# Rotary tables in two steps, a second norm gathered in one slot, and another start of the first expert, in a two-layer attention and expert kernel on one core

## The chip, the core and the metric

The kernel runs on one core of a Trainium2 chip. A core has five engines with a queue of instructions each: PE (TensorE, matmuls and transposes, into PSUM), DVE (VectorE) and ACT (ScalarE) for arithmetic on SBUF and PSUM, POOL (GpSimd), and SP, which here only issues DMAs. Engines run side by side and wait for each other through semaphores. An instruction that waits holds up all that stands behind it in its own queue. The metric is the device time of one execution in microseconds (us), lower is better; it is given as the median of several runs.

## The reference

The input is `x`, 4 sequences of 512 rows of 512 numbers, and a context of 4 x 64 rows. Two layers follow each other, each an attention and a feed-forward part, each added to `x` through a gate:

```
x = x + tanh(g_xattn[0]) * L0_xattn(layernorm(x), ctx, ...)
x = x + tanh(g_ffn[0])   * L0_ffn(layernorm(x), ...)
x = x + tanh(g_xattn[1]) * L1_xattn(layernorm(x), ctx, mask, ...)
x = x + tanh(g_ffn[1])   * L1_ffn(layernorm(x), ...)
```

`L0_xattn` has 16 query heads and 4 key heads of 128. Queries and keys are normed, scaled by `q_norm_w` and `k_norm_w` and rotated: `q * cos + rotate_half(q) * sin`. The keys and values are those of the 64 context rows and, under a causal mask, of the 512 rows of the sequence itself. `L0_ffn` is a shared network plus a routed one: each of the 2048 rows goes to 4 of 16 experts, an expert takes up to 256 rows, and its weighted output is added to the row. The change lies in these first two parts and in what joins them. The second layer is not touched.

## The kernel before

`x` stays in SBUF as `x_res`, 16 tiles of 128 rows. The program is a chain of stages, and a stage ends with its semaphores cleared and a barrier of all engines (`Scope.clear`, line 98). Three stages matter here.

**`attention0_stage`** (names `a_...`). A step is one key head and one tile of rows, 4 x 16 = 64 steps, and the work of a step is spread over several *slots*. Slots are numbered from -3 to 65. Strings of words (`PE_ORDER`, `ACT_ORDER`, `DVE_ORDER`, `POOL_ORDER`, lines 133 to 159) say by hand what each engine does in a slot, and in which order. Slots -3 to -1 and the first are written out, the others go by the slot's number modulo 4. The words used below:

- `Z`, `C`, `c`, `H`, `G`: the context, in two batches 0 and 1. `C` multiplies a batch's rows into keys in a bank of `a_A`. On DVE `c` sums the squares (L654) and takes the keys out of the bank (L655). On POOL `c` is three instructions (L768, L770, L773) that make the norm. `H` turns the normed keys (L823), `G` makes the values (L817).
- `b`, `t` on DVE: `b` scales the keys' norm weight; `t` multiplies the loaded cosines and sines with the norm weights of keys and queries, two tables `a_cos_k`, `a_cos_q` (L645) and two tables `a_sin_k`, `a_sin_q` (L648, four instructions of 128 columns each), and casts the causal mask (L650).
- `k`, `q`: projections to key and value and to the queries, each number split into a high and a low half, so three matmuls for one (lines 120 to 122). The two banks of `a_A` are taken in turn by `C`, `k`, `q`, `G`, `V` and `W`. The first `q` takes the bank of the second `C`, and so waits for L655 of batch 1.
- `f` on ACT squares the queries (L599); `E` on DVE sums them (L713) and rotates (L714, L717); `q` on POOL norms and adds (L747 to L755); `K` and `T` on PE turn keys and queries (L904, L909).
- `A` on DVE (L616 to L620), `r` on POOL (L731), `X` on DVE (L629), `R` on PE (L830) and `r` on ACT (L515): the layer norm of a tile of `x`: sums, `rstd`, normed rows `a_xn`, transposes, and the copy into `xT`. `row(s, ahead, i)` says which tile is due in a slot. Tiles 0 to 3 are done at once in slot -3, tiles 4 to 15 one in a slot. Tile numbers 16 to 19 are the *second* norm, that of the first four tiles of `x` after this attention, for the next stage. They stand in slots 60 to 64, one in a slot, between the work of the last steps.
- `S`, `M`, `e`, `P`, `g`, `V`, `o`, `B`, `W`, `D`: scores, their maxima, exponentials, transposes of the probabilities and their copies, the product with the values, its split in two halves (L578 on ACT, L699 on DVE), the output projection, and the sum into `x` (L695).

**`ffn0_front_stage`** (`m_...`) computes the shared network and the routing, and writes the rows of `x` to `y_rows` in device memory. Its SP queue ends with waits for these writes (`y_stored`) and for the normed rows (`stored`).

**`experts_stage`** (`e_...`) runs 16 experts. ACT copies an expert's weights into a high half `e_whi` in three pieces (gate, up, down; L1673), POOL makes the low halves `e_wlo` of gate and up (L1503), DVE that of down (L1735). PE turns the gathered rows into `e_TR` (L1540), ACT and DVE split them (`split_x`, L1679 and L1728), and the matmuls into `e_GUP` follow. For the first expert the queues are filled by these lines of ACT:

```
                for j in range(NW):
                    split_hi(0, j)
                split_x(0)
```

Of the kernel before, what the change touches and what calls it, by code (L numbers as in the profile page):

```python
# [24 lines left out]
F32 = mybir.dt.float32  # L25
# [99 lines left out]
def attention0_stage(nc, x, ident, tri, gates, xT, xh, xl, next_weights, next_loaded, xn_dram, x_in, ctx_in, wq_in, wk_in, wv_in, wo_in, wkc_in, wvc_in, qw_in, kw_in, g_xattn, g_ffn,  # L125
# [7 lines left out]
    PE_ORDER = {-3: "Z0 Z1 R0 R1 R2 R3 C0 C1",  # L133
# [10 lines left out]
    ACT_ORDER = {-3: "z0 z1 r0 r1 r2 r3 x u w c0",  # L144
# [13 lines left out]
    POOL_ORDER = {-3: "r0 r1 r2 r3 x w c0", -2: "x c1 r", -1: "q x r", "first": "x q p0 p1 r",  # L158
# [15 lines left out]
    def steps(order, s):  # L174
        return [(word[0], int(word[1:] or 0)) for word in order[s if s < 0 else s % BT if s > 0 else "first"].split()]
# [91 lines left out]
    with ExitStack() as ctx:  # L267
# [99 lines left out]
        with nc.Block() as block:  # L367
# [133 lines left out]
            def _(act):  # L501
# [3 lines left out]
                def do(name, i, s, m):  # L505
# [99 lines left out]
            def _(ve):  # L605
                ve.memset(mhalf[:], -0.5).then_inc(tab_ready, 1)
                ve.memset(heps[:], HD * 1e-6).then_inc(tab_ready, 1)
                def do(name, i, s, m):
# [12 lines left out]
                    if name == "X" and row(s, 5, i) is not None:  # L621
# [19 lines left out]
                    if name == "t":  # L641

                        ve.wait_ge(tab_loaded, 48)
                        for q, wr in (("k", kw[:]), ("q", wrow[:, 0])):
                            ve.tensor_tensor(cw[q][:], cw["q"][:], wr.unsqueeze(1).broadcast_to([P, BT, HD]), ALU.mult).then_inc(tab_ready, 1)  # L645
                            swapped = wr.rearrange("p (s d) -> p s d", s=2)[:, ::-1, :]
                            for t in range(BT):
# [1928 lines left out]
```

## Time and profile before

| | |
|---|---|
| median of 3 runs | 1999.44 us (1999.3 to 1999.74) |
| the profiled execution | 1994.72 us |
| its span, first to last instruction | 1992.9 us |
| PE busy (share of the span) | 1852.5 us (93%) |
| DVE busy | 1099.0 us (55%) |
| ACT busy | 1038.4 us (52%) |
| POOL busy | 962.9 us (48%) |

The shares are means over all stages. The profile is read by stretch: a table of the engines' busy time in a stretch, the instructions in order of time, and for each of them the idle time of its engine just before and what ended it. An idle time of PE that ends with another engine's instruction names the chain that was late there.

### The profile page before, as it was taken

How to read it: one execution, taken by the hardware profiler on the slowest of the kernel's cores; microseconds unless marked ns; L12 is line 12 of the kernel's file. 1: busy time of each engine (PE TensorE's matmuls, PEld its weight loads, DVE VectorE, ACT ScalarE, POOL GpSimd, SP SyncE). 2: the span in 40 equal slices, each digit the busy share in tenths (PEclk: the TensorE clock that was granted, in tenths of full speed). 3: DMA queues.
4: the chain of work that ended last, by engine and by line, in shares of the span. 5: the costliest groups of instructions: out<-in, count | busy, mean ns of one | idle time of the engine just before them, and what ended most of it. 6: DMA issues, size and time to landing. Idle time of an engine off the chain costs nothing. (4 is left out here: it accounts for less than half of the span.)

```text
span 1992.9 us, 27633 instructions
## 1 busy us (share of the span) xinstructions
PE 1852.5 (93%) x9796; PEld 1323.4 (66%) x9796; DVE 1099.0 (55%) x2264; ACT 1038.4 (52%) x2251; POOL 962.9 (48%) x865
## 2 busy tenths in 40 slices
PE   6999999999999999999998999989999778859998
PEld 4666766766766666666765877769999656624443
DVE  4544544446455654556444648424343678748886
ACT  3555656554554545544544321126666367647775
POOL 4544565444653445544531100028888355537774
PEclk8999999999999999999999999989999989979999
DMA  7111111111012111111011100147889750000000
GB/s 235 45 50 50 48 34 47 62 31 50 34 33 71 48 52 47 34 49 39 25 47 67 65 22 22 43 144 203 233 226 273 184 134 1 1 0 23 21 18 27
DMA packets 112952, 141.18 MB, mean 71 GB/s; under 512 B 37408, under 2 KB 68128, under 8 KB 112624
## 3 DMA queue, kind: packets, MB, share of 16 engines
q1 hardware_dynamic: 105648, 122.63, 19.6%
q0 software_dynamic: 7168, 16.78, 4.0%
q8 instruction: 80, 1.31, 0.3%
q14 instruction: 56, 0.46, 0.1%
HBM read 104.78 MB, written 29.36 MB: 67 GB/s over the span
## 5 line engine op out<-in xcount | busy, mean ns | idle before, releaser
L743 POOL TENSOR_TENSOR a_xcl<-xT,a_xch 128x512 fp32r<-128x512 f32 x64 | 82.4, 1287 | 322.9 <-ACT a_xch L558 322.9
L898 PE MATMUL a_A<-a_pT,a_vf 128*128 128x512 f32 (+1 forms) x448 | 236.7, 610 | 0.9 <-ACT a_pT L574 0.9
L848 PE MATMUL a_S<-a_kT,a_qT 128*128 128x288 f32 (+3 forms) x640 | 209.7, 426 | 4.8 <-ACT a_qT L586 3.1
L659 DVE TENSOR_REDUCE a_nmax<-a_S 128x1 f32<-128x192 f32 (+3 forms) x256 | 138.1, 551 | 83.2 <-PE a_S L849 81.9
L564 ACT ACTIVATE a_pr_odd<-a_S,a_nmax 128x320 f32<-128x320 f32 (+1 forms) x128 | 80.9, 633 | 156.1 <-DVE a_nmax L659 154.8
L120 PE MATMUL a_A<-a_wlo,a_xch 128*128 128x512 f32 x256 | 153.7, 600 | 6.3 <-DVE a_qT L655 6.3
L848 PEld LDWEIGHTS a_S<-a_kT,a_qT 128*128 128x128 f32 x640 | 114.8, 189 | 53.8 <-issue 26.8
L574 ACT ACTIVATE a_pT<-a_TR 128x512 f32<-128x512 f32 (+1 forms) x224 | 132.3, 591 | 33.0 <-PE a_TR L888 32.2
L2404 PE MATMUL f_HH<-w12T,f_f_xqT 128*128 128x512 bf16 x512 | 125.0, 394 | 14.8 <-DVE f_h L2261 13.0
L564 ACT ACTIVATE a_pr_even<-a_S,a_nmax 128x192 f32<-128x192 f32 (+1 forms) x128 | 67.0, 525 | 135.1 <-DVE a_nmax L659 135.0
L1503 POOL TENSOR_TENSOR e_wlo<-expert_raw,e_whi 128x1408 fp32r<-128x1408 f32 x32 | 102.8, 3232 | 68.0 <-ACT e_whi L1673 68.0
L699 DVE TENSOR_TENSOR a_otl<-a_A,a_oth 128x512 fp32r<-128x512 f32 x64 | 44.2, 691 | 152.1 <-ACT a_oth L578 152.1
L120 PE MATMUL a_A<-a_wlo,a_oth 128*128 128x512 f32 x256 | 111.4, 435 | 7.3 <-DVE a_otl L699 7.2
L120 PE MATMUL e_GUP<-e_xgl,e_whi 128*128 128x256 f32 (+1 forms) x384 | 110.8, 289 | 5.2 <-DVE e_xgl L1728 4.5
L121 PE MATMUL e_GUP<-e_xgh,e_wlo 128*128 128x256 f32 (+1 forms) x384 | 109.3, 285 | 0.0
L122 PE MATMUL e_GUP<-e_xgh,e_whi 128*128 128x256 f32 (+1 forms) x384 | 108.7, 283 | 0.0
L2041 POOL TENSOR_TENSOR f_hg<-f_h,g 128x512 f32<-128x512 f32 x64 | 81.4, 1272 | 51.8 <-DVE f_h L2261 51.8
L122 PE MATMUL a_A<-a_whi,a_xch 128*128 128x512 f32 x256 | 102.2, 399 | 0.0
L121 PE MATMUL a_A<-a_whi,a_xcl 128*128 128x512 f32 x256 | 102.0, 398 | 0.0
L122 PE MATMUL a_A<-a_whi,a_oth 128*128 128x512 f32 x256 | 101.6, 397 | 0.0
L121 PE MATMUL a_A<-a_whi,a_otl 128*128 128x512 f32 x256 | 101.1, 395 | 0.0
L684 DVE RECIPROCAL a_rec<-a_rs 128x1 f32<-128x1 f32 x256 | 41.3, 161 | 107.7 <-ACT a_pr_odd L564 57.6
(389 smaller groups left out, 5193.3 us busy)
## 6 DMA issues: line engine op xcount, KB each, us to landing
a_pw<-in_L_ffn_w_dram SPq DMA_DIRECT2D x96, 256.0 KB, 2.8
expert_raw<-in_L_ffn_w_gate_dram SPq DMA_DIRECT2D x16, 704.0 KB, 7.9
expert_raw<-in_L_ffn_w_up_dram SPq DMA_DIRECT2D x16, 704.0 KB, 9.8
expert_raw<-in_L_ffn_w_down_dram SPq DMA_DIRECT2D x16, 512.0 KB, 10.2
tern<-a_tern SPq DMA_DIRECT2D x48, 128.0 KB, 1.9
x_res<-in_x_dram SPq DMA_DIRECT2D x4, 1024.0 KB, 9.3
a_raw<-in_L_xattn_wq_dram SPq DMA_DIRECT2D x4, 1024.0 KB, 6.5
a_raw<-in_L_xattn_wo_dram SPq DMA_DIRECT2D x4, 1024.0 KB, 5.5
```

The source lines that it names most:

```text
L120: pe.matmul(out, lhs_hi, rhs_lo, start=first, stop=False)
L121: pe.matmul(out, lhs_lo, rhs_hi, start=False, stop=False)
L122: return pe.matmul(out, lhs_hi, rhs_hi, start=False, stop=last)
L564: act.activation(pr[s % 2][:, i, 0:keys(s)], pair(s, i), ACT.Exp, bias=nmax[:, s % 2, i:i + 1], accum_out=rs[:, s % 2, i:i + 1]).then_inc( ...
L574: act.activation(pT[0:rows(i), i % 2], TR[0:rows(i), TR_USE["P", t, i][0]], ACT.Copy).then_inc(pT_ready, 1)
L659: ve.tensor_reduce(nmax[:, s % 2, i:i + 1], pair(s, i), AX.X, ALU.max, negate=True).then_inc(s_max, 1)
L743: pool.tensor_tensor(xcl[:, t % 2], xT[:, :, tok(t)], xch[:, t % 2].bitcast(F32), ALU.subtract).then_inc(xlo_ready, 1)
L848: pe.matmul(bank[:, lo:hi], qT[:, t % 2, hq], kT[:, par(t), lo:hi], start=True, stop=hi < nk)
L898: last = pe.matmul(A[:, A_USE["V", t, 0][0]], vf[r, par(t), i], pT[r, i % 2], start=i == 0, stop=i == nkt - 1)
L1503: pool.tensor_tensor(wlo[e % 2][q, cs], raw[q, e % 2, cs], whi[e % 2][q, cs].bitcast(F32), ALU.subtract).then_inc(gu_lo, 1)
L2041: pool.tensor_tensor(hg[:, u, part(n)], h[:, u, part(n)], g3[:, part(n)], ALU.mult).then_inc(hg_ready, 1)
L2404: last = pe.matmul(HH[pair_of(s, n)][j][:], f_xqT[:, u, j * KD + k], w12T[j][:, k, part(n)], start=k == 0, stop=k == KD - 1)
```

## The change

There are four parts.

1. **Tables.** The word `t` is split into `t0` (keys) and `t1` (queries and mask). `t0` stands ahead of `c1` as before, `t1` behind it. The four sine instructions of a table become one of 512 columns. In slot -2 DVE's order `v E A` becomes `v A E`.
2. **Second norm.** Slot 64 gets an order of its own, `"last"`, in which all four tiles 16 to 19 are normed. Slots 60 to 63 have none of it. The transposes go into the score banks `a_S` instead of `a_TR`, and DVE copies them into `xT` instead of ACT.
3. **Stores of the front stage.** `y_stored` outlives the stage. The waits at the end of its SP queue are gone; SP and POOL wait for `y_stored` in the experts' stage, where they first need it.
4. **First expert.** ACT splits the rows after the first weight piece instead of after the third. DVE makes the low half of the gate piece, and POOL only that of the up piece.

```diff
-    PE_ORDER = {-3: "Z0 Z1 R0 R1 R2 R3 C0 C1",
+    PE_ORDER = {"last": "W0 W1 W2 W3 R0 P0 P1 V0 R1 P2 V1 P3 V2 R2 P4 V3 R3 V4", -3: "Z0 Z1 R0 R1 R2 R3 C0 C1",
...
-    ACT_ORDER = {-3: "z0 z1 r0 r1 r2 r3 x u w c0",
+    ACT_ORDER = {"last": "g0 g1 g2 g3 g4 o L", -3: "z0 z1 r0 r1 r2 r3 x u w c0",
...
-    DVE_ORDER = {-3: "A0 A1 X0 A2 X1 A3 X2 X3 b u c0 t c1", -2: "v E A", -1: "v X E A", "first": DVE_SLOT,
+    DVE_ORDER = {"last": "A0 A1 X0 D X1 r0 A2 X2 r1 A3 X3 r2 r3 B", -3: "A0 A1 X0 A2 X1 A3 X2 X3 b u c0 t0 c1 t1", -2: "v A E", -1: "v X E A", "first": DVE_SLOT,
...
+                    if name == "r":
+                        t = row(s, 5, i)
+                        ve.wait_ge(xn_turned, t + 1)
+                        ve.wait_ge(xlo_ready, SLOTS)
+                        ve.tensor_copy(xT[:, :, tok(t)], S[:, i].rearrange("p (k t) -> p k t", k=KD)).then_inc(xT_ready, 1)
...
-                            for t in range(BT):
-                                ve.tensor_tensor(sw[q][:, t], sw["q"][:, t], swapped, ALU.mult).then_inc(tab_ready, 1)
+                        ve.tensor_tensor(sw[q][:], sw["q"][:], swapped, ALU.mult).then_inc(tab_ready, 1)
...
-                        bank = bank_of_TR("R", t, 0, s, m)
+                        if s == SLOTS:
+                            pe.wait_ge(s_exp, GH * SLOTS)
+                            bank = S[:, i]
+                        else:
+                            bank = bank_of_TR("R", t, 0, s, m)
...
-                for r in range(RING):
-                    sp.wait_ge(stored[r], 16 * (NT - BT) // RING)
-                sp.wait_ge(y_stored, 16 * (NT + 2 * NS))
...
+                sp.wait_ge(y_stored, 16 * (NT + 2 * NS))
                 for e in range(2, E):
...
-                    for j in range(2):
+                    for j in (1,) if e == 0 else range(2):
                         pool.wait_ge(whi_ready, NW * e + j + 1)
+                        pool.wait_ge(gu_lo, 2 * e + j)
...
+                    else:
+                        pool.wait_ge(y_stored, 16 * (NT + 2 * NS))
...
-                for j in range(NW):
+                split_hi(0, 0)
+                split_x(0)
+                for j in range(1, NW):
                     split_hi(0, j)
-                split_x(0)
...
+                ve.wait_ge(whi_ready, 1)
+                for q, cs in pieces(0):
+                    ve.tensor_tensor(wlo[0][q, cs], raw[q, 0, cs], whi[0][q, cs].bitcast(F32), ALU.subtract).then_inc(gu_lo, 1)
                 split_x(0)
```

DVE in the opening, before: `a_ssc` and `a_qT` are the `c` of one batch, `a_kT` is where the loaded mask lies, the instructions with `a_ssq` and behind it are `E`, and `a_stats` to `a_veps` are `A`.

```order
L645 TENSOR_TENSOR a_cos_k<-a_cos_q,a_kw 128x512
L648 TENSOR_TENSOR a_sin_k<-a_sin_q,a_kw 128x128 x4
L645 TENSOR_TENSOR a_cos_q<-a_cos_q,a_sq 128x512
L648 TENSOR_TENSOR a_sin_q<-a_sin_q,a_sq 128x128 x4
L650 CAST a_causal<-a_kT 128x128
L654 TENSOR_REDUCE a_ssc<-a_pr_even 128x4
L655 TENSOR_TENSOR a_qT<-a_A,a_kw 128x512
L704 TENSOR_TENSOR a_qa<-a_A,a_cos_k 128x128
L706 TENSOR_TENSOR a_qb<-a_A,a_sin_k 128x128
L713 TENSOR_REDUCE a_ssq<-a_sq 128x5
L714 TENSOR_TENSOR a_qa<-a_A,a_cos_q 128x512
L717 TENSOR_TENSOR a_qb<-a_A,a_sin_q 128x512
```

The same place on DVE in the changed kernel:

```order
L652 TENSOR_TENSOR a_cos_k<-a_cos_q,a_kw 128x512
L654 TENSOR_TENSOR a_sin_k<-a_sin_q,a_kw 128x512
L661 TENSOR_REDUCE a_ssc<-a_pr_even 128x4
L662 TENSOR_TENSOR a_qT<-a_A,a_kw 128x512
L652 TENSOR_TENSOR a_cos_q<-a_cos_q,a_sq 128x512
L654 TENSOR_TENSOR a_sin_q<-a_sin_q,a_sq 128x512
L657 CAST a_causal<-a_kT 128x128
L711 TENSOR_TENSOR a_qa<-a_A,a_cos_k 128x128
L713 TENSOR_TENSOR a_qb<-a_A,a_sin_k 128x128
L617 BN_STATS a_stats<-x_res 128x6
L619 BN_AGGR a_mv<-a_stats 128x2
L621 TENSOR_SCALAR a_veps<-a_mv 128x1
```

The second batch of the context moved ahead of the query tables and the mask, and `A` ahead of `E`.

PE in slot 64, behind its `W`, before: `a_pr_odd` rows are `P`, `a_vf` rows are `V`, the `a_xn` row is the `R` of tile 19.

```order
L888 MATMUL a_TR<-ident_f,a_pr_odd 128x128 x4
L830 MATMUL a_TR<-ident_f,a_xn 128x128 x4
L888 MATMUL a_TR<-ident_f,a_pr_odd 128x128 x4
L898 MATMUL a_A<-a_pT,a_vf 128x512
L888 MATMUL a_TR<-ident_f,a_pr_odd 128x128 x4
L898 MATMUL a_A<-a_pT,a_vf 128x512
L888 MATMUL a_TR<-ident_f,a_pr_odd 128x128 x4
L898 MATMUL a_A<-a_pT,a_vf 128x512
L888 MATMUL a_TR<-ident_f,a_pr_odd 128x128 x4
L898 MATMUL a_A<-a_pT,a_vf 128x512 x2
```

The same place on PE in the changed kernel:

```order
L841 MATMUL a_S<-ident_f,a_xn 128x128 x4
L899 MATMUL a_TR<-ident_f,a_pr_odd 128x128 x8
L909 MATMUL a_A<-a_pT,a_vf 128x512
L841 MATMUL a_S<-ident_f,a_xn 128x128 x4
L899 MATMUL a_TR<-ident_f,a_pr_odd 128x128 x4
L909 MATMUL a_A<-a_pT,a_vf 128x512
L899 MATMUL a_TR<-ident_f,a_pr_odd 128x128 x4
L909 MATMUL a_A<-a_pT,a_vf 128x512
L841 MATMUL a_S<-ident_f,a_xn 128x128 x4
L899 MATMUL a_TR<-ident_f,a_pr_odd 128x128 x4
L909 MATMUL a_A<-a_pT,a_vf 128x512
L841 MATMUL a_S<-ident_f,a_xn 128x128 x4
```

Three groups of transposes came in from slots 61 to 63, where nothing stands in their place.

ACT at the start of the experts, before (`expert_raw` are the loaded weights):

```order
L1673 ACTIVATE e_whi<-expert_raw 128x1408 x2
L1673 ACTIVATE e_whi<-expert_raw 128x1024
L1673 ACTIVATE e_whi<-expert_raw 96x512
L1679 ACTIVATE e_xgh<-e_TR 128x4x128 x2
L1698 ACTIVATE e_sil<-e_GUP 128x256
```

The same place on ACT in the changed kernel:

```order
L1685 ACTIVATE e_whi<-expert_raw 128x1408
L1691 ACTIVATE e_xgh<-e_TR 128x4x128 x2
L1685 ACTIVATE e_whi<-expert_raw 128x1408
L1685 ACTIVATE e_whi<-expert_raw 128x1024
L1685 ACTIVATE e_whi<-expert_raw 96x512
L1711 ACTIVATE e_sil<-e_GUP 128x256
```

The split of the rows moved ahead of the up and down pieces.

## Rows read from the trace of the kernel before

**Rows 1.** Stretches: length, busy us (instructions) per engine, PE's granted clock, DMA share, GB/s
```profile
80.00:1010.00 930.00, 913.11 (x4456) 642.49 (x4455) 485.19 (x1068) 502.12 (x1264) 452.57 (x445) 1.00 0.15 47
...
44.40:47.80 3.40, 3.38 (x11) 2.87 (x11) 0.00 (x0) 1.19 (x2) 0.44 (x1) 0.51 0.05 14
```

**Rows 2.** DVE in time, opening: start, us, line, output<-inputs, count [idle <-releaser]
```profile
20.41 0.68 DVE L645 TENSOR_TENSOR a_cos_k<-a_cos_q,a_kw 128x512 f32<-128x512 f32 x1
21.01 3.06 DVE L648 TENSOR_TENSOR a_sin_k<-a_sin_q,a_kw 128x128 f32<-128x128 f32 x4
...
28.16 0.68 DVE L655 TENSOR_TENSOR a_qT<-a_A,a_kw 128x512 f32<-128x512 f32 x1
...
21.01 1.38 DVE L648 TENSOR_TENSOR a_sin_k<-a_sin_q,a_kw 128x128 f32<-128x128 f32 x1
```

**Rows 3.** PE and ACT in time, opening
```profile
28.90 0.79 PE L120 MATMUL a_A<-a_wlo,a_xch 128*128 128x512 f32 x1 [6.34 <-DVE a_qT L655]
...
34.88 0.60 ACT L599 ACTIVATE a_sq<-a_A 128x512 f32<-128x512 f32 x1 [1.57 <-PE a_A L122]
...
37.68 0.67 PE L817 MATMUL a_A<-a_pT,a_pr_even 128*128 128x512 f32 x1 [0.96 <-DVE a_qb L717]
...
43.66 0.33 PE L904 MATMUL a_TR<-ident_f,a_qa 128*128 128x128 f32 x1 [2.32 <-POOL a_qa L755]
```

**Rows 4.** POOL in time, opening
```profile
20.43 1.81 POOL L738 TENSOR_TENSOR a_wlo<-a_raw,a_whi 128x512 fp32r<-128x512 f32 x1
...
22.20 1.31 POOL L738 TENSOR_TENSOR a_wlo<-a_raw,a_whi 128x512 fp32r<-128x512 f32 x1
...
25.09 1.09 POOL L773 TENSOR_TENSOR a_qT<-a_qT,a_src 128x512 f32<-128x512 f32 x1
...
38.61 0.56 POOL L731 TENSOR_TENSOR a_rstd<-a_veps,a_mhalf 128x1 f32<-128x1 f32 x1 [7.81 <-DVE a_veps L620]
...
42.35 1.25 POOL L755 TENSOR_TENSOR a_qa<-a_qa,a_srq 128x640 f32<-128x640 f32 x1
```

**Rows 5.** Issue of x's second batch, in time, and its landing, KB, us
```profile
17.12 0.47 SPq L394 DMA_DIRECT2D x_res<-in_x_dram  x1
...
x_res<-in_x_dram SPq DMA_DIRECT2D x1, 1024.0 KB, 8.2
```

**Rows 6.** Slots 61 to 65: group (count, busy us, mean ns, idle before), then in time
```profile
L830 PE MATMUL a_TR<-ident_f,a_xn 128*128 128x128 f32 x16 | 2.6, 283 | 2.3 <-DVE a_xn L629 2.3
...
1067.53 0.68 DVE L616 BATCH_NORM_STATS2 a_stats<-x_res 128x6 f32<-128x512 f32 x1
...
1068.70 0.56 POOL L731 TENSOR_TENSOR a_rstd<-a_veps,a_mhalf 128x1 f32<-128x1 f32 x1 [8.52 <-DVE a_veps L620]
...
1079.19 0.60 ACT L578 ACTIVATE a_oth<-a_A 128x512 fp32r<-128x512 f32 x1 [1.22 <-PE a_A L898]
```

**Rows 7.** Last store of the front stage, in time, and its landing, KB, us
```profile
1326.33 0.32 SPq L1027 DMA_DIRECT2D y_rows<-x_res  x1
...
y_rows<-x_res SPq DMA_DIRECT2D x1, 256.0 KB, 2.0
```

**Rows 8.** Start of the experts in time; last, a subtraction of the front stage
```profile
1329.49 4.11 ACT L1673 ACTIVATE e_whi<-expert_raw 128x1408 fp32r<-128x1408 f32 x4 [19.80 <-PEq L100]
1329.51 1.94 PE L1540 MATMUL e_TR<-ident_f,xg 128*128 128x128 f32 x8 [4.00 <-PEq L100]
1330.95 6.27 POOL L1503 TENSOR_TENSOR e_wlo<-expert_raw,e_whi 128x1408 fp32r<-128x1408 f32 x2 [47.79 <-ACT e_whi L1673]
...
1334.59 1.29 DVE L1728 TENSOR_TENSOR e_xgl<-e_TR,e_xgh 128x512 fp32r<-128x512 f32 x2 [8.29 <-ACT e_xgh L1679]
...
1335.94 0.58 PE L120 MATMUL e_GUP<-e_xgl,e_whi 128*128 128x256 f32 x1 [4.49 <-DVE e_xgl L1728]
...
1341.46 0.38 ACT L1698 ACTIVATE e_sil<-e_GUP 128x256 f32<-128x256 f32 x1 [6.90 <-PE e_GUP L122]
...
1086.55 3.30 DVE L1216 TENSOR_TENSOR m_gl<-xT,m_gh 128x704 fp32r<-128x704 f32 x4 [0.71 <-ACT m_gh L1157]
```

More of the change, by code:

```diff
@@ L174, in steps @@
     def steps(order, s):
-        return [(word[0], int(word[1:] or 0)) for word in order[s if s < 0 else s % BT if s > 0 else "first"].split()]
+        kind = s if s < 0 else "first" if s == 0 else "last" if s == SLOTS else s % BT
+        return [(word[0], int(word[1:] or 0)) for word in order[kind].split()]
     def batch_next(s):
@@ L184, in row @@
             return i
-        n = s + ahead
-        return n if BT <= n < PERIOD else n - AGAIN if PERIOD <= n - AGAIN < PERIOD + BT else None
+        if s == SLOTS:
+            return PERIOD + i
+        return s + ahead if BT <= s + ahead < PERIOD else None
     def bank_order(firsts):
@@ L197, in bank_order @@
                 elif name == "R":
-                    if row(s, 5, i) is not None:
+                    if s < SLOTS and row(s, 5, i) is not None:
                         taken.append((name, row(s, 5, i), 0))
@@ L509, in do @@
                                        ACT.Copy).then_inc(ctx_copied, 1)
-                    if name == "r" and row(s, 5, i) is not None:
+                    if name == "r" and s < SLOTS and row(s, 5, i) is not None:
                         t = row(s, 5, i)
                         act.wait_ge(xn_turned, t + 1)
-                        if t >= PERIOD:
-                            act.wait_ge(xlo_ready, SLOTS)
                         act.activation(xT[:, :, tok(t)], TR[:, TR_USE["R", t, 0][0]].rearrange("p (k t) -> p k t", k=KD),
@@ L641, in do @@
                     if name == "t":
[L643 to L646, printed above, removed]
[L647 to L651 removed]
+                        if i == 0:
+                            ve.wait_ge(tab_loaded, 48)
+                        q, wr = (("k", kw[:]), ("q", wrow[:, 0]))[i]
+                        ve.tensor_tensor(cw[q][:], cw["q"][:], wr.unsqueeze(1).broadcast_to([P, BT, HD]), ALU.mult).then_inc(tab_ready, 1)
+                        swapped = wr.rearrange("p (s d) -> p s d", s=2)[:, ::-1, :].unsqueeze(1).broadcast_to([P, BT, 2, HD // 2])
+                        ve.tensor_tensor(sw[q][:], sw["q"][:], swapped, ALU.mult).then_inc(tab_ready, 1)
+                        if i == 1:
+                            ve.wait_ge(causal_loaded, 16)
+                            ve.tensor_copy(causal[:], causal_in).then_inc(tab_ready, 1)
+                            ve.wait_ge(tab_ready, TABLES)
                     if name == "c":
```

23 lines of the change are left out of this document (10 added, 13 removed), and 2 rows, old and new, of the table ACT_ORDER.

## The prediction

> **What bounds the kernel now.** I read the table of stretches first, then PE's instructions in time with the idle time ahead of each, then for each idle time the instruction that ended it, on its own engine. From 80 to 1010 us PE is busy 913.11 of 930 us at a full granted clock [rows 1]: nothing is to be had there, and the change doesn't touch it. What it touches are three places where PE stands still.
>
> *Opening.* PE waits 6.34 us for L655, ready only at 28.84 because DVE does all the tables ahead of it [rows 2, 3]. It waits again, 2.32 us, until 43.66, for POOL's last instruction on the first queries [rows 3]. POOL began that chain at 39.17, behind an `rstd` for which it had waited 7.81 us; the DVE sums under that `rstd` stand behind `E` [rows 4]. Right after this idle time PE's clock was granted at 0.51, the 1.2 GHz level, from 44.4 to 47.8 [rows 1].
>
> *Last slots.* In slots 61 to 65 PE waits 2.3 us in all for normed rows of the second norm [rows 6].
>
> *From front stage to experts.* The last row store is issued at 1326.33 and lands 2.0 us later, at 1328.33; only then does SP reach the barrier [rows 7], and ACT and PE begin at 1329.49 [rows 8]. PE's first expert matmul starts 6.45 us after that: ACT first copies all three weight pieces (4.11 us), then splits the rows, and DVE follows [rows 8].
>
> **Part 1, the tables.** DVE does the key cosines at 20.41 (0.68 us for 512 columns). The first sine piece of 128 columns, at 21.01, took 1.38 us, until 22.39; POOL's weight chunk had ended at 22.24 [rows 2, 4]. I read this as DVE held until the chunk was over. One sine instruction of 512 columns is in neither kernel's trace so far. Not held it would end at 21.7; held as the first piece was, and then as long as the cosine one, at 22.9; as long as the four together at 24.07. I take 22.9, the nearest row being the same operation at the same place. POOL's fourth chunk (1.31) then ends at 24.2 instead of 23.51. `c1` follows on DVE, two instructions of 0.68 with some overlap, 1.3 in all: the bank is free at 24.2, and PE goes on at 24.25 instead of 28.90, **4.65 us sooner**.
>
> From there the chain is the old one. PE's restart to `f` on ACT took 34.88 - 28.90 = 5.98: `f` at 30.25. `G0` followed `f` by 2.80: at 33.05. It took 43.66 - 2.32 - 37.68 = 3.66 [rows 3]: PE could start `K` at 36.7. POOL must be as quick: from its fourth chunk to the end of the first batch's norm took 26.18 - 23.51 = 2.67 [rows 4], so 26.9; a subtraction of a chunk's size, 1.3, to 28.2; the second batch, again 2.67, to 30.9; the `rstd`, 0.56, to 31.45, since its sums now stand ahead of `E`. The query chain starts with DVE's sum behind `f`: 30.25 + 0.60 + an estimated 0.85 (640 columns at the rate of 0.68 for 512) = 31.7. It took 42.35 + 1.25 - 39.17 = 4.43 [rows 4], which gives 36.15. So `K` comes at 36.75 instead of 43.66: **6.9 us**, with PE's second idle time gone.
>
> Then the clock. The 3.4 us at 0.51 would be 1.7 at the full clock. The idle time just ahead of them is gone, but another, of some 0.4, stands at 30.5. I take 1.1 of the 1.7, between none and all. **Opening: 8.0 us**, bounds 4.6 (only the first idle time) and 9.2 (all of the clock, and a little of the matmuls behind 28.90 that ran slow).
>
> What the swapped `A` adds is a wait of DVE for `x`'s second batch, with `E` queued behind it and POOL and PE behind that. It is issued at 17.12 and lands 8.2 later, at 25.3 [rows 5]; DVE gets there at about 26.5. No cost. The query tables and the mask (two of 0.68 and a cast) run from 24.2 to about 26 and are needed by `f` at 30.25: hidden, with 4 us to spare.
>
> **Part 2, the second norm.** PE does the same 16 transposes of 283 ns [rows 6], only later, and ACT's four copies become four on DVE (0.68 each by L655, which reads PSUM too). So PE's work is neither more nor less, and what goes are the waits, 2.3 us, and some 0.2 for banks that the transposes shared with the probabilities: **2.5 us**, if slot 64 makes no new wait. There DVE does per tile the sums (1068.70 - 1067.53 = 1.17 until POOL can start), POOL 0.56 [rows 6], then `X` (an estimated 0.55) and the copy 0.68: about 3.0 us in a row for a tile. The first `X` stands ahead of `D` and is ready 1.17 + 0.56 + 0.55 = 2.3 after the slot's start, the second, behind `D`, at an estimated 4.3, and the fourth at about 4.3 + 2 x 3.0 = 10.3. PE comes to the fourth transposes behind V3. In the old slot `o` started 11.66 after the start [rows 6], so V3 ended near 10.5 less the old wait, plus the two groups of transposes put in: near 10.7. The margin is 0.4 us. Behind the fourth stand V4, `o`, `B` and the last `W`, all on the path. `X2` and `X3` also wait for the stores of `X0` and `X1`; at 2.0 for such a store [rows 7] these land at about 5.1 and 6.7, ahead of need. Bounds: 0.8 (DVE 1.7 late) to 3.2.
>
> **Part 3, the stores.** The barrier came 1329.49 - 1328.33 = 1.16 ahead of the next stage's work [rows 7, 8]. Now SP is free when its last issue ends, 1326.65, so work starts at 1327.81: 1.68 less, I take **1.6**, bounds 1.0 and 1.7. SP's new wait stands ahead of the load of the third expert, POOL's ahead of its first add; both come later than 1328.33 by more than the time of a store. No cost.
>
> **Part 4, the first expert**, counted from the start of ACT [rows 8]. Gate piece: 4.11 us are for 4352 columns, so 1408 take 1.33. The transposes end at 1.96; ACT splits the rows by 3.0 (it took 1334.59 - 1333.60 = 1.0). DVE makes the gate's low half from 1.33: 704 columns took 0.83, so 1.65, to 3.0, while POOL is idle; then `split_x`, 1.29, to 4.3. PE starts at 4.35 instead of 6.45. Up piece: ACT from 3.0 to 4.35, POOL 3.13 more, 7.5. PE's first group took 5.52 from its start to ACT's L1698, half of it gate: 2.76, so at 7.1 PE waits 0.4 for up. Gain 2.1 - 0.4 = 1.7; less if these matmuls are a little quicker and the wait longer: **1.5**, bounds 0.5 and 2.1. DVE's down piece now waits behind POOL, but is needed only by the second product, several us later.
>
> **Sum.** 8.0 + 2.5 + 1.6 + 1.5 = 13.6 us off the profiled execution's 1994.72: 1981.1. The median of the runs is 1999.44, 4.7 above that execution, and I take the difference off it: **1985.8 us**. All four places are ahead of barriers or on a chain through PE, and the loads in between are started by progress, not by the clock on the wall, so I expect no later place to take the gain back.
>
> **Rivals.**
>
> *POOL becomes the bound of the opening.* The chunk that began just as DVE did its cosines took 1.81, the next 1.31 [rows 4]: a DVE instruction held POOL for 0.5. In the new order the two query tables and the cast run beside POOL's norm of the context. Three times 0.5 puts `K` 1.5 later, PE waits again, and the clock falls as before (1.1): opening 5.4, time 1988.4. Against it: POOL's chain ends 0.6 ahead of need. Chance 0.16. The Trainium skill (SBUF — State Buffer, Who interferes with whom) says that a VectorE instruction with two SBUF inputs holds GpSimd's reads of SBUF for its whole length, and that issue order decides who waits. By that the three would cost 0.68 each, 2.0 in all, and the time would be 1988.9; the trace agrees in kind, with 0.5 for 0.68.
>
> *The norms crowd slot 64.* DVE's chain is late by 2.5 us, through `X` waiting for a port or a store, and `o` with it: part 2 gives nothing, 1988.3. For it: a margin of 0.4. Against it: POOL has nothing else to do there. Chance 0.10.
>
> *The sine instruction does not do what it should*: held again in between, it ends at 24.07. Then PE restarts 1.2 later, 1987.0. Chance 0.06.
>
> *Two of these at once, and a smaller part missing too*: a gain under 4.0 us, about 1996. Chance 0.04.
>
> *Slower than before*: DVE waits in `A` for `x`'s second batch with `E` behind it. `E` is due at 30.85 and `A` takes 1.2, so from a landing after 29.7 on each us costs one. It uses up all 13.6 at a landing at 43.3; at 48 the time is 2004. It landed at 25.3 [rows 5]. Chance 0.02.
>
> **How the numbers follow.** My forecast has 0.62, the rivals the rest. The time is the forecast's, 1985.8. The bounds of the terms give 16.2 us at best (1983.2) and 6.9 at worst (1992.5). The range runs from 1983.2 to 1991.2, which takes in the first three rivals, the first two together as well (1990.9), and leaves out less than 2 in 10. A measurement of this kernel can tell 0.2%, 4.0 us, from no change. Faster by more: 0.62 + 0.16 + 0.10 + 0.06 = 0.94, of which I give 0.01 to within, for a forecast that fails wholly: 0.93; within: 0.04 + 0.01 = 0.05; slower: 0.02.
>
> **What would show it.** Right: PE's first long idle time ends near 24.2, on L662; `K` starts near 36.7 with little or no wait on POOL; no wait of PE for `a_xn` in slots 61 to 63, and `o` of slot 64 about 12 us after the slot's start; 2.5 us instead of 4.0 of idle PE ahead of `e_TR`; PE's first expert matmul 4.35 after ACT's start, with a short wait before the up half. Wrong: PE idle ahead of `K` as long as before, or ahead of V4 or the last `W`; a wait of DVE for `x` in the opening; a first group of the expert that waits for POOL by more than 1.5.

## The result and the profile after

| | before | changed |
|---|---|---|
| first comparison, median | 1999.59 us (4 runs, 1999.30 to 1999.99) | 1983.91 us (4 runs, 1979.17 to 1984.32) |
| all runs whose clock is on record, mean | 1997.5 us (58 runs, 1991.5 to 2001.7) | 1983.4 us (10 runs, 1979.2 to 1985.3) |
| mean granted clock of PE over those runs | 0.9752 | 0.9781 |

The ratio of the first comparison is 0.9916 (0.9899 to 0.9933), a gain of 16.8 us (13.4 to 20.2). Over the runs of the second row the gain is 14.1 us, with an interval of 1.3 to either side. The forecast was 13.6 and 1985.8. The direction was right; by the first ratio the time is 0.9916 x 1999.44 = 1982.6, 0.6 under the lower end of the range (the ten runs' mean, 1983.4, lies just inside it). Both kernels turned out to have a spread of 6 to 10 us, of which the three runs shown of before had told nothing.

The profiled execution of the changed kernel took 1984.32 us (span 1982.5). PE, opening, in time order: start, length, line, output<-inputs, count, and in brackets the idle time just before and what ended it.

```profile
24.99 0.50 PE L120 MATMUL a_A<-a_wlo,a_xch 128*128 128x512 f32 x1 [2.63 <-DVE a_qT L662]
...
30.61 0.66 PE L830 MATMUL a_TR<-ident_f,a_qT 128*128 128x128 f32 x4 [0.54 <-POOL a_qT L780]
32.90 1.96 PE L824 MATMUL a_A<-a_pT,a_pr_even 128*128 128x512 f32 x4 [0.20 <-DVE a_qb L724]
...
36.41 0.27 PE L915 MATMUL a_TR<-ident_f,a_qa 128*128 128x128 f32 x1
...
40.77 0.49 PE L859 MATMUL a_S<-a_kT,a_qT 128*128 128x192 f32 x2
```

The 6.34 us ahead of 28.90 [rows 3] have become 2.63 ahead of 24.99, and the 2.32 ahead of `K` are gone: `K` (L915) starts at 36.41 instead of 43.66, 7.25 sooner (forecast 6.9). A new short wait stands at 30.61, for POOL's norm of the second batch of the context. DVE and POOL in the same stretch:

```profile
20.29 1.77 DVE L652 TENSOR_TENSOR a_cos_k<-a_cos_q,a_kw 128x512 f32<-128x512 f32 x1
21.99 1.75 DVE L654 TENSOR_TENSOR a_sin_k<-a_sin_q,a_kw 128x512 f32<-128x512 f32 x1
...
28.64 0.68 DVE L617 BATCH_NORM_STATS2 a_stats<-x_res 128x6 f32<-128x512 f32 x1
```

```profile
20.23 1.28 POOL L745 TENSOR_TENSOR a_wlo<-a_raw,a_whi 128x512 fp32r<-128x512 f32 x1
...
30.52 0.56 POOL L738 TENSOR_TENSOR a_rstd<-a_veps,a_mhalf 128x1 f32<-128x1 f32 x1
```

The one sine instruction took 1.75, as near to a held one as was forecast, but the cosine ahead of it, 0.68 before [rows 2], took 1.77. `A` (L617) ran without a wait for `x`, and the `rstd` at 30.52 had nothing to wait for, where it had waited 7.81 [rows 4]. PE's clock was not full here either: it was granted at 0.51 from 25.5 to 28.8, behind the wait of 2.63.

Slots 61 to 65, PE's transposes of normed rows as a group (count, busy us, mean ns, idle ahead), and the table of two stretches (length, busy time of PE, PEld, DVE, ACT and POOL, granted clock, DMA share, GB/s):

```profile
L841 PE MATMUL a_S<-ident_f,a_xn 128*128 128x128 f32 x16 | 2.5, 276 | 0.0
```

```profile
1056.30:1059.60 3.30, 3.30 (x10) 2.52 (x9) 1.91 (x7) 0.00 (x0) 1.37 (x2) 0.51 0.15 48
...
1060.36:1076.03 15.67, 11.81 (x59) 7.57 (x57) 10.46 (x18) 5.36 (x8) 1.10 (x2) 1.00 0.14 52
```

The 2.3 us of waiting [rows 6] are 0.0. But for 3.3 us at the start of slot 64 PE's clock was at 0.51, the 1.2 GHz level, which it was not in the trace of before.

From the front stage into the experts, in time:

```profile
1317.05 0.32 SPq L1037 DMA_DIRECT2D y_rows<-x_res  x1
1318.45 1.38 ACT L1685 ACTIVATE e_whi<-expert_raw 128x1408 fp32r<-128x1408 f32 x1 [18.04 <-PEq L100]
1318.47 1.27 PE L1552 MATMUL e_TR<-ident_f,xg 128*128 128x128 f32 x8 [2.24 <-PEq L100]
1319.78 1.08 ACT L1691 ACTIVATE e_xgh<-e_TR 128x512 fp32r<-128x512 f32 x2
1319.86 1.63 DVE L1797 TENSOR_TENSOR e_wlo<-expert_raw,e_whi 128x1408 fp32r<-128x1408 f32 x1 [2.84 <-ACT e_whi L1685]
...
1322.21 3.18 POOL L1513 TENSOR_TENSOR e_wlo<-expert_raw,e_whi 128x1408 fp32r<-128x1408 f32 x1 [48.33 <-ACT e_whi L1685]
1322.74 0.58 PE L120 MATMUL e_GUP<-e_xgl,e_whi 128*128 128x256 f32 x1 [2.99 <-DVE e_xgl L1741]
...
1327.42 0.38 ACT L1711 ACTIVATE e_sil<-e_GUP 128x256 f32<-128x256 f32 x1 [3.83 <-PE e_GUP L122]
```

From the last store's issue to ACT it is 1.40 us instead of 3.16 [rows 7, 8], and PE's first expert matmul comes 4.29 after ACT's start (forecast 4.35) instead of 6.45. The first activation comes 8.97 after it instead of 11.97, 3.0 sooner, where 1.5 was forecast.

### The profile page after: what moved, and what is told of

Its sections match the earlier page's. It is cut to its first block and busy times, and to the rows that moved or that the text cites. A ratio compares the mean times of both kernels' runs of the same rounds, so it can differ in the third digit from the quotient of the medians.

```text
span 1982.5 us, 27619 instructions
## 1 busy us (share of the span) xinstructions
PE 1847.9 (93%) x9759; PEld 1322.3 (67%) x9796; DVE 1103.4 (56%) x2263; ACT 1037.7 (52%) x2247; POOL 960.6 (48%) x864
## 5 line engine op out<-in xcount | busy, mean ns | idle before, releaser
L575 ACT ACTIVATE a_pT<-a_TR 128x512 f32<-128x512 f32 (+1 forms) x224 | 132.3, 591 | 37.2 <-PE a_TR L899 36.4
```

Of the source, the lines that this page charges most:

```text
L575: act.activation(pT[0:rows(i), i % 2], TR[0:rows(i), TR_USE["P", t, i][0]], ACT.Copy).then_inc(pT_ready, 1)
```

## The experiments

**The four parts apart.** Each stands alone in the kernel before, as in the change's diff; of each edit one place is shown here.

```diff
-... b u c0 t c1", -2: "v E A"                        # p1_tables
+... b u c0 t0 c1 t1", -2: "v A E"
```

> Part 1 alone (tables, second keys, A ahead of E) in the kernel before. In the changed kernel the first score matmul came at 40.77 instead of 49.28, 8.5 us sooner, and from slot 20 to slot 60 the lead stayed at 8.25 to 8.36. Theory 'sum of places': the whole program gains that, 8.3 us (1991.2 against 1999.5), and the profile shows the score matmul near 40.8. Theory 'clock decides': the place gains 8.3 but the stretches at the 1.2 GHz level fall elsewhere behind it, so that the time differs from 1991.2 by one or more steps of 1.7 us (3.4 us at 0.5 for 1.7 us of work). The term of the prediction was 8.0.

Measured: 0.9950 (0.9935 to 0.9964), median 1990.89 (6 runs) against 1998.88. The first score matmul, `S`, came at 40.76, where it had come at 49.28: as in the changed kernel (40.77).

```diff
+    DVE_ORDER = {"last": "A0 A1 X0 D X1 r0 A2 X2 r1 A3 X3 r2 r3 B", ...   # p2_norm
```

> Part 2 alone (second norm all in slot 64) in the kernel before. In the changed kernel PE's lead grew by 3.4 us in slots 61 to 63, then shrank by 1.7 in slot 64, where PE's clock was granted at 0.5 for 3.4 us beside the output projection, and by a little more at the transposes. Theory 'sum of places': without a fall of the clock in slot 64 the gain is about 3.0 (1996.5), with one 1.3 (1998.2); the next stage begins 3.0 or 1.3 sooner. Theory 'DVE crowds slot 64' (a rival of the prediction): PE waits ahead of V4 or of the last W by 2 us and the gain is under 1. The term of the prediction was 2.5.

Measured: 0.9985 (0.9975 to 0.9995), median 1995.67 (12 runs).

```diff
-                sp.wait_ge(y_stored, 16 * (NT + 2 * NS))   # front stage, p3_stores
+                sp.wait_ge(y_stored, 16 * (NT + 2 * NS))   # experts' stage
```

> Part 3 alone (the front stage's last waits moved into the experts' stage). Theory 'sum of places': idle time of PE ahead of the first expert transposes 2.2 us instead of 4.0, gain 1.75 (1997.75). Rival 'given back': the wait for the stores comes back as a wait of SP or POOL in the experts' stage or as a later fall of the clock, and the gain is 0 to 0.5. The term of the prediction was 1.6.

Measured: 0.9973 (0.9957 to 0.9990), median 1993.63 (8 runs). The idle time ahead of the transposes was 2.24.

```diff
+                split_hi(0, 0)                             # p4_first
+                split_x(0)
```

> Part 4 alone (first expert: rows split after the gate piece, gate's low half on DVE). In the changed kernel PE's first expert matmul came 4.3 us after ACT's start instead of 6.45, there was no wait for the up half, and the stretch at 0.5 of the clock there was 6.8 us long instead of 13.7. Theory 'wait and clock': 2.15 for the wait plus about 0.85 for matmuls at the full clock, gain 3.0 (1996.5); the wait is worth more than itself because an idle PE is followed by a slow one. Theory 'wait alone' (the prediction's step, 2.1 less a wait for the up half): gain 1.5 (1998.0), the low clock as long as before.

Measured: 0.9991 (0.9981 to 1.0002), median 1997.12 (12 runs).

The medians' gains add up to 18.2 us and contradict the traces: part 3 removes 1.8 us at its place and seems to gain 5.3. The trace of part 3 shows why. Up to 1321 us its program is that of before, instruction for instruction. One stretch in both traces, first before, then with part 3 alone (the second trace is 4.3 us ahead here):

```profile
580.00:600.00 20.00, 18.07 (x78) 11.47 (x76) 12.93 (x24) 10.03 (x27) 14.62 (x14) 0.91 0.13 40
```

```profile
580.00:600.00 20.00, 17.17 (x80) 11.07 (x78) 14.16 (x25) 9.98 (x26) 12.57 (x11) 1.00 0.26 81
```

In one execution the clock fell to the lower level in there, in the other nowhere between 110 and 1000 us; through this and like places in the opening the trace with part 3 was 5.8 us ahead of that of before at the 58th `D` (988.38 against 994.16), where not one instruction differs yet. So a single trace, or a handful of runs, compares two draws of the clock besides two kernels. The Trainium skill (TensorE: Matmul & The Clock Gate, What's actually happening) says that the gate runs on its own time and does not start over with a kernel; these two traces are in keeping with it, but do not prove it.

The sizes were therefore taken by place: the time between the same two instructions in every trace, compared where the clock's share is alike or as a mean over traces. A trace counts as unchanged in a row if its kernel lacks the part that acts at that place, so that the trace with part 1 alone is a changed one in the first row and an unchanged one in the last.

| place | unchanged | changed | gain | forecast |
|---|---|---|---|---|
| start to first `D` (L702) | 82.8, 81.4, 78.5, 83.0; mean 81.4 | 74.5, 74.5, 72.3, 74.1, 72.7, 72.2; mean 73.4 | 8.0 | 8.0 |
| 58th `D` to first weight piece of the front stage, clock full | 91.56, 91.57 | 88.64 to 88.66 (five traces) | 2.9 | 2.5 |
| the same with one fall of the clock | 93.14, 93.14 | 90.22 to 90.23 (four traces) | 2.9 | |
| last store's issue to ACT's start | 3.15 to 3.16 | 1.40 | 1.75 | 1.6 |
| ACT's start to seventh L1715 (the third expert's first) | 40.79, 40.87, 39.58; mean 40.4 | 37.67 to 37.70 (four traces) | 2.7 | 1.5 |

The first row has the traces of before and of parts 2, 3 and 4 alone, and six with part 1 as it is in the change. The first and the last row also hold differences of the clock. In the opening the four unchanged traces had 6.8 to 17.1 us at the lower level, the six changed ones 0 to 10.2, so the 8.0 is the difference of two means with a wide spread; up to `K` alone the means are 43.4 and 36.2, a gain of 7.2, and the other 0.8 lies behind `K`.

The falls in slot 64 came with the old and the new slot alike, and cost 1.58 in both: they are no effect of part 2. The sum by place is 15.4, the mean of the runs gives 14.1.

**The changed kernel once more, and three steps undone in it.**

> The changed kernel once more, unaltered. Theory 'clock decides the spread': the places show the same gaps as in the first trace (first long idle time of PE ends at 25.0, the first expert matmul comes 4.3 us after ACT's start), but the stretches at the 1.2 GHz level stand elsewhere, and the runs spread by some 8 us as those of the kernel before do (1991.8 to 2001.7). The ratio comes out nearer to what the four parts give apart at equal mean clock (12.4 us together, by a line through all runs) plus a share for the clock: 12 to 16 us. Rival 'the gain is larger than its places': 16 to 20 us and something behind the experts is shorter in the trace.

Measured: 0.9944 (0.9927 to 0.9962), median 1983.83 (6 runs). The places repeat to 0.02 us where the clock does; this time it was full in the whole opening (first row, granted clock 1.00; second row, the same stretch in the first trace, 0.85), and then PE waited longer for POOL:

```profile
25.00:36.00 11.00, 8.91 (x40) 5.89 (x41) 7.64 (x14) 2.76 (x6) 10.57 (x11) 1.00 0.84 282
```

```profile
24.99:36.41 11.42, 10.68 (x40) 7.24 (x41) 8.30 (x14) 2.76 (x6) 10.42 (x11) 0.85 0.79 273
```

```profile
30.64 0.65 PE L830 MATMUL a_TR<-ident_f,a_qT 128*128 128x128 f32 x4 [2.09 <-POOL a_qT L780]
36.00 0.27 PE L915 MATMUL a_TR<-ident_f,a_qa 128*128 128x128 f32 x1
```

A faster PE gains 0.4 at `K`: POOL, busy for 10.57 of 11.00 us, bounds this stretch.

```diff
-    "... c0 t0 c1 t1", -2: "v A E"      # a1_E_A
+    "... c0 t0 c1 t1", -2: "v E A"
```

> The changed kernel with E ahead of A again in slot -2 on DVE. Theory (the prediction's step): the rstd of POOL waits for A behind E, so POOL's query chain starts at 34.4 instead of 31.6 and K comes at 38.8 instead of 36.4, with an idle time of PE of about 2.4 us ahead of it; the place loses 2.4, and perhaps a further 1.7 by the clock after the idle time. Rival 'the swap is worth nothing': K stays at 36.4 to 36.8, because G0 or the chunk of POOL ends last there anyway.

Measured by 7 runs: 0.9947 (0.9931 to 0.9963), median 1984.93. POOL and PE:

```profile
34.05 0.56 POOL L738 TENSOR_TENSOR a_rstd<-a_veps,a_mhalf 128x1 f32<-128x1 f32 x1 [3.18 <-DVE a_veps L621]
```

```profile
39.10 0.33 PE L915 MATMUL a_TR<-ident_f,a_qa 128*128 128x128 f32 x1 [2.32 <-POOL a_qa L762]
```

The old wait of 2.32 is back, to the hundredth, and `K` comes 2.4 later (its trace starts 0.3 later too). So two words in another order are worth 2.4 us of the opening. The times alone couldn't have told. The further loss by the clock, which I had thought possible, did not come: with the wait back, the clock was at 1.00 from 39.1 to 50.0. The fall that stood behind this wait at 44.4 [rows 1] is thus not brought by the wait alone; it is absent with part 3 alone too, where the wait is 2.32 as well. What else it needs is open.

```diff
-                        ve.tensor_tensor(sw[q][:], sw["q"][:], swapped, ALU.mult)      # a2_four
+                        for t in range(BT):
+                            ve.tensor_tensor(sw[q][:, t], sw["q"][:, t], swapped, ALU.mult)
```

> The changed kernel with each sine table in four instructions of 128 columns again, the order left as it is. In the first trace of the changed kernel the key cosines took 1.77 us instead of 0.68 and the one sine instruction 1.75, 3.45 together from 20.29 to 23.74; four pieces after a cosine of 0.68 took 3.66 in all in the kernel before. Theory 'order alone': the step from four to one is worth 0.2 us or nothing, PE restarts at 25.0 to 25.3 and K comes at 36.4 to 36.7. Theory 'one step' (the prediction's, 1.2 for it): PE restarts at about 26.1.

Measured: 0.9931 (0.9908 to 0.9954), median 1980.78 (4 runs).

```profile
20.44 1.76 DVE L652 TENSOR_TENSOR a_cos_k<-a_cos_q,a_kw 128x512 f32<-128x512 f32 x1
22.12 1.96 DVE L655 TENSOR_TENSOR a_sin_k<-a_sin_q,a_kw 128x128 f32<-128x128 f32 x4
```

```profile
25.33 0.50 PE L120 MATMUL a_A<-a_wlo,a_xch 128*128 128x512 f32 x1 [2.83 <-DVE a_qT L663]
```

Four sines take 1.96, one takes 1.75: the step is worth 0.2, and PE restarts at 25.33 (25.2 when the start of this trace is taken off). In these traces, where POOL's chunk began ahead of the cosine, the order of the words is the gain and the one instruction is not; the next kernel has another case.

```diff
-                ve.wait_ge(whi_ready, 1)     # and DVE's low half of the gate; a4_pool
-                    for j in (1,) if e == 0 else range(2):
+                    for j in range(2):
```

> The changed kernel, but the gate's low half of the first expert is made by POOL again, ahead of the up half; ACT's new order stays. Theory 'the helper is needed': DVE is free for the split of the rows, so PE's first expert matmul comes 3.7 us after ACT's start instead of 4.3, but POOL ends the up half at about 7.7 instead of 6.9 and PE waits about 1 us ahead of the up half or for the gate's low half; the first activation of the gate comes 8.8 to 9.5 after the start, against 9.0 in the changed kernel: a loss of 0 to 0.8 us at the place. Rival: POOL keeps up, and DVE's part of the change was not needed: the first activation comes at 8.4 and the place gains 0.6.

Measured: 0.9917 (0.9894 to 0.9940), median 1978.32 (4 runs), the fastest median so far. In the trace the place is slower:

```profile
1314.05 1.38 ACT L1683 ACTIVATE e_whi<-expert_raw 128x1408 fp32r<-128x1408 f32 x1 [18.04 <-PEq L100]
...
1315.52 6.30 POOL L1511 TENSOR_TENSOR e_wlo<-expert_raw,e_whi 128x1408 fp32r<-128x1408 f32 x2 [46.04 <-ACT e_whi L1683]
...
1318.82 0.55 PE L120 MATMUL e_GUP<-e_xgl,e_whi 128*128 128x256 f32 x1 [3.49 <-POOL e_wlo L1511]
...
1323.61 0.38 ACT L1709 ACTIVATE e_sil<-e_GUP 128x256 f32<-128x256 f32 x1 [4.43 <-PE e_GUP L122]
```

PE waits for POOL's gate half until 4.77 after ACT's start, and the first activation comes at 9.56 instead of 8.97: DVE's help is worth 0.6. The median is lower all the same, at a mean clock of 0.9815 over these runs against 0.9781. In the trace the gain lies where nothing was edited: from the first `D` to the last store, and from the last expert to the end, it is together 6.6 us shorter than the second trace of the changed kernel, with 14.7 us less at the lower level.

The opening is the changed kernel's, but in this trace the cosine began ahead of POOL's chunk:

```profile
20.62 0.79 DVE L652 TENSOR_TENSOR a_cos_k<-a_cos_q,a_kw 128x512 f32<-128x512 f32 x1
20.83 1.74 POOL L745 TENSOR_TENSOR a_wlo<-a_raw,a_whi 128x512 fp32r<-128x512 f32 x1
...
21.34 1.78 DVE L654 TENSOR_TENSOR a_sin_k<-a_sin_q,a_kw 128x512 f32<-128x512 f32 x1
...
24.37 0.50 PE L120 MATMUL a_A<-a_wlo,a_xch 128*128 128x512 f32 x1 [1.41 <-DVE a_qT L662]
```

Cosine and sine take 2.50 here instead of 3.45, where the kernel before needed 3.66 with the cosine ahead too, and PE waits 1.41 instead of 2.63. So the one instruction can be worth 1.2 at the end of the key tables. `K` gained nothing by it: it came at 36.09, and at 36.00 in the second trace of the changed kernel, both with a full clock up to there.

**Why the first expert gained more than forecast.**

```diff
+                for r in range(RING):                                  # a5_no3: part 3 undone
+                    sp.wait_ge(stored[r], 16 * (NT - BT) // RING)
+                sp.wait_ge(y_stored, 16 * (NT + 2 * NS))
```

> The changed kernel with part 3 undone: the waits for the stores stand at the end of the front stage again. Cut by place (from ACT's first weight piece to the seventh write of the expert's hidden rows' high half, that is some three experts), the start of the experts took 40.8, 40.9, 39.6 and 40.1 us in four traces without part 4, 38.9 with part 4 alone and 37.7 in five traces with parts 3 and 4. Theory 'parts 3 and 4 share a gain': the shorter idle time ahead of the first transposes also shortens the stretch at the 1.2 GHz level that follows, so that here, with part 4 but without part 3, the start takes 38.9 again (a stretch of 9 to 10 us at 0.5) and the idle time ahead is 4.0 instead of 2.2: 3.0 us lost at this place in all. Rival 'parts are independent': the start takes 37.7 as in the changed kernel and only the 1.75 of the idle time is lost. By all runs the time is 1.75 to 3.0 above the changed kernel's, whose ten runs have a mean of 1983.4: 1985.1 to 1986.4, if the clock is as kind elsewhere.

Measured: 0.9946 (0.9930 to 0.9961), median 1985.56 (6 runs). The start of the experts took 38.66. The first 14 us from ACT's start, as the table of stretches gives them (PE's busy time is first, the granted clock third from the end): before, part 1 alone (here as before), part 3 alone, this kernel, the changed kernel.

```profile
1329.49:1343.49 14.00, 9.49 (x50) 9.11 (x51) 5.44 (x7) 6.60 (x9) 8.99 (x4) 0.57 0.25 81
```

```profile
1323.55:1337.55 14.00, 9.49 (x60) 9.11 (x61) 5.44 (x7) 7.37 (x10) 9.51 (x5) 0.66 0.25 81
```

```profile
1321.95:1335.95 14.00, 9.30 (x56) 8.92 (x57) 5.45 (x7) 7.11 (x9) 9.02 (x4) 0.63 0.27 85
```

```profile
1314.35:1328.35 14.00, 11.18 (x68) 10.51 (x69) 7.95 (x9) 7.92 (x12) 7.37 (x4) 0.68 0.27 84
```

```profile
1318.45:1332.45 14.00, 10.99 (x77) 10.53 (x78) 8.26 (x10) 8.86 (x12) 8.33 (x4) 0.76 0.32 106
```

PE stood still, ahead of its first transposes and again ahead of its first matmul, for 4.0 + 4.5 us before and with part 1, 2.2 + 4.7 with part 3, 4.0 + 2.5 with part 4, and 2.2 + 3.0 with both. The granted clock is 0.57 and 0.66 with the same idle times, so the 0.63 of part 3 alone and the 0.66 and 0.68 of part 4 without part 3 show little by themselves. With both parts it was 0.76 in each of six traces. The place took 40.1 us with part 3 alone, which can't be told from the 39.6 to 40.9 without either. Part 4 without part 3 takes 38.7 to 38.9 us, some 1.6 less than the mean of 40.4 without either, near the forecast's 1.5. Part 3 then adds 1.75 ahead of the place and another 1.0 to 1.2 in it: the stretch at the lower level is 8.9 and 9.5 us long in the two traces without it and 6.8 with it, and half of that difference is 1.0 to 1.3. The rival 'parts are independent' is refuted for part 3 on top of part 4; what part 3 does to the clock alone is open. That the idle time is the cause was tried with work that does nothing but fill it:

```diff
                 turn(0)
+                for n in range(14):                                    # e_fill
+                    pe.transpose(M[:, n % 2, 0:P], ident[:], ident[:])
```

> The changed kernel with 14 transposes of the identity more on PE, written to a bank that is overwritten later, between the first expert's transposes and its first matmul. They do no useful work; they fill the 3.0 us for which PE stands still there. In five traces with parts 3 and 4 the 14 us from ACT's first weight piece hold 6.8 us at the 1.2 GHz level, and the start of the experts takes 37.7 us. Theory 'an idle PE is followed by a slow one': with an idle time of under 1 us there the stretch is gone or half as long, the first matmuls run at 0.14 us instead of 0.21 a piece, PE then waits for POOL's up half (ready at 6.9 us), and the start takes 36.7 to 37.2 us. Rival 'it follows the barrier': the idle time of 2.2 us ahead of the first transposes brings the stretch, which stays 6.8 us long, and the start takes 37.7 as before.

Measured: 0.9913 (0.9899 to 0.9927), median 1981.21 (5 runs).

```profile
1316.31:1330.31 14.00, 12.93 (x93) 12.35 (x94) 8.28 (x10) 9.09 (x12) 8.61 (x4) 0.88 0.32 108
```

```profile
1317.36 3.19 PE L1604 MATMUL e_M<-ident_f 128*128 128x128 f32 x14
...
1323.28 0.39 PE L120 MATMUL e_GUP<-e_xgl,e_whi 128*128 128x256 f32 x1 [0.99 <-POOL e_wlo L1513]
```

The clock is at 0.88 in this one trace, where it was 0.76 in all six without the filling, so the idle time between transposes and matmuls does bring part of the slow stretch. But only 0.3 us are gained (37.38 against 37.68): PE now waits 0.99 for POOL's up half, which takes back more than I had expected (36.7 to 37.2 for the place). The stretch was halved, not removed; what the remaining idle time ahead of the transposes adds wasn't tried.

**A further step.**

```diff
-    "... c0 t0 c1 t1"      # best
+    "... c0 c1 t0 t1"
+                pool.tensor_tensor(wlo[0][:, GU // 2:GU], ...).then_inc(gate_half, 1)
```

> The changed kernel with two small steps more. First, the context's second keys stand ahead of both tables on DVE (c0 c1 t0 t1): PE should restart at 23.0 instead of 25.0. Second, the gate's low half of the first expert is shared: DVE makes columns 0 to 703, POOL 704 to 1407. Theory 'POOL and f bound the opening next': POOL ends its query chain only about 0.5 us sooner, because the rstd and f (which waits for the query tables and the mask) are next, so K comes at 35.8 to 36.2 instead of 36.4. Rival 'the first bank bounds it': K comes at 34.5 to 35.0. Theory 'DVE and POOL get in each other's way': the DVE half takes as long as POOL's, 1.5 to 1.6 us instead of 0.8, and the first expert matmul stays at 4.3 us after ACT's start. Rival: it comes at 3.7 to 3.8, and the place gains 0.5. In all 0.3 to 2.4 us off the changed kernel, too little to be told by the times, so the traces decide by place.

Measured: 0.9924 (0.9908 to 0.9941), median 1983.18 (6 runs, mean 1982.3): not to be told from the changed kernel. PE and DVE in the opening:

```profile
23.38 0.50 PE L120 MATMUL a_A<-a_wlo,a_xch 128*128 128x512 f32 x1 [0.58 <-DVE a_qT L662]
...
30.22 0.66 PE L830 MATMUL a_TR<-ident_f,a_qT 128*128 128x128 f32 x4 [2.08 <-POOL a_qT L780]
37.17 0.27 PE L915 MATMUL a_TR<-ident_f,a_qa 128*128 128x128 f32 x1
```

```profile
23.24 0.68 DVE L652 TENSOR_TENSOR a_cos_k<-a_cos_q,a_kw 128x512 f32<-128x512 f32 x1
23.84 0.68 DVE L654 TENSOR_TENSOR a_sin_k<-a_sin_q,a_kw 128x512 f32<-128x512 f32 x1
```

PE restarts 1.6 us sooner and gains 0.4 at L830, where it waits for POOL again. `K` itself came at 37.17, later than in the changed kernel (36.41 and 36.00) and than in both expectations; in this trace the clock fell just behind that wait, from 31.2 to 34.6, where PE has no wait left to make up for it. In the first expert, the first matmul came 3.98 after ACT's start, between the two expectations, and the place took 37.68, as in the changed kernel: PE waits 0.26 for POOL's up half. Neither step gained anything in the end.

## Why the prediction was right or wrong

**Opening: 8.0 forecast, 8.0 by place.** That the two agree to a tenth is luck, as the traces of one kernel lie 2 us and more apart there. `K` was forecast 6.9 sooner and came 7.2 sooner on average. The 1.1 for the clock has 0.8 against it, but not by the mechanism given: the fall at 44.4 was there in three of four unchanged traces and in no changed one, yet it did not return with the wait in front of it.

The way to `K` was right in part. PE's restart gained 3.91 instead of 4.65. What was off is the held instruction: I let one sine be held by one chunk of POOL. In the first trace cosine and sine were each held, because POOL's chunk began at 20.23, 0.06 ahead of the cosine at 20.29. Before, the cosine began at 20.41, 0.02 ahead of POOL's chunk at 20.43, and it was POOL that was held, to 1.81 [rows 2, 4]. In the kernel `best`, behind all of POOL's chunks, cosine and sine took 0.68 each. The Trainium skill (SBUF — State Buffer, Who interferes with whom) says that the order of issue decides who of VectorE and GpSimd is blocked; these three traces agree, and I had used the rule for the rival but not for the sum. Which of the two begins first differs between executions of the same opening: in the trace of `a4_pool` it was the cosine, and the key tables took 2.50, the forecast's length (20.41 to 22.9). The rest of the path made good for it. In the first trace `f` came at 30.11 (forecast 30.25), POOL's second norm ended at 30.56 (30.9), `K` at 36.41 (36.75). The swap of `A` and `E` did what was forecast, shown by undoing it.

**The rival 'POOL becomes the bound'** came about, at L830 rather than at `K`: 0.54 us of waiting with a slow PE, 2.09 with a fast one. I had weighed POOL's chain only against `K`. The gain was not lost by it: `K` came at 36.41 and 36.00 in these two traces.

**Last slots: 2.5 forecast, 2.9 measured.** No wait for normed rows was left, and DVE was not late: `o` stood 13.7 us behind the start of slot 64 in the first trace, 1.6 of it from the clock. The rival 'norms crowd slot 64' is refuted.

**Stores: 1.6 forecast, 1.75 measured.** SP and POOL show no wait for `y_stored`.

**First expert: 1.5 forecast, 2.7 measured by place, 3.0 to the first activation in the first pair of traces. This is the step that failed.** The path was right (4.29 against 4.35), but I ended it at the wait for the up half, put the clock at nothing, and added parts 3 and 4 as if they were independent. One shortens PE's idle time ahead of the transposes, the other that behind them. With part 4 in place, part 3 made the slow stretch 2.1 to 2.7 us shorter and gained 1.0 to 1.2 at a place where I had given it nothing; the filled gap shows that idle time of PE there lengthens the slow stretch. In the opening I had priced the clock; here, where the first matmul of [rows 8] took 0.58 (0.28 further on, at the full clock), I had not. The 0.4 for the up half did not come either: PE was still slow enough to meet POOL's end.

**The sum and the range.** The terms 8.0 + 2.5 + 1.6 + 1.5 became 8.0 + 2.9 + 1.75 + 2.7 = 15.4 by place and 14.1 by the runs' means, so the 13.6 was 0.5 to 1.8 short. Of the 3.2 us between 1985.8 and 1982.6 the terms by place make 1.8; 15.4 off the median before would still be 1984.0, inside the range. The other 1.4 is the base. I took the 4.7 us between profile and median as a fixed remainder and three runs within 0.44 us as the kernel's spread; 58 runs spread by 10 us, with a mean 2.0 below that median. The stretch from the last L1715 to the end, mostly the second layer and unchanged, took between 434.5 and 440.6 us in the thirteen traces. So on which side of the range's lower end a handful of runs falls is a draw of the clock. The range was made of the terms' bounds only; with the clock's part, estimated from the 6 to 10 us of spread, it would have had to reach some 3 us lower.

**Later places** took nothing back: from the third to the last expert all traces agree within 0.03 us (188.11 to 188.14).

## What to carry to other kernels

When a wait of PE goes, look at the clock in the stretch behind it: an edit that shortens an idle time can gain once more there (here 1.0 to 1.2 us on top of 1.75), and the next engine in line (here POOL) takes what is left. Size an edit of 1 to 3 us by the time between two fixed instructions in several traces, not by medians of a few runs. Where VectorE and GpSimd both read SBUF, read from several traces which of them starts first, since 0.06 us decided who lost 1.1, and one kernel showed both orders.

## What the runs showed that was not expected

- The same instructions ran at a granted clock of 0.91 in one execution and 1.00 in another, in a stretch where PE was busy for 90% of the time (580 to 600 us); a fall cost about 1.5 us at its place. The kernel before spread from 1991.5 to 2001.7, with mean clocks of 0.979 in its faster runs down to 0.971 in its slower ones.
- Fourteen transposes that compute nothing raised the clock of the 14 us from 0.76 to 0.88 (one trace), and gained 0.3 us.
- A cosine of 512 columns took 0.68 or 1.77 us, depending on 0.06 us of who began first. In the kernel before that changed nothing at the end of the four sine pieces: from the cosine's start to there it took 3.66 with DVE first, and 3.63 and 3.69 in the traces of parts 3 and 4 alone, with POOL first.
